# A delta-rule kernel: products of the solved group's last two channel blocks dealt out between value projections instead of a block behind them

## The chip, the cores and the metric

The kernel runs on one core of one Trainium2 chip. The metric is the device time of one execution in microseconds (us); lower is better. The core has five engines with queues of their own: TensorE (PE, with its weight loads shown as PEld), VectorE (DVE), ScalarE (ACT), GpSimd (POOL) and SyncE (SP), which issues the transfers.

## The reference, cut to what matters

A residual block over x of 128 sequences x 32 tokens x 512 channels: a cross attention, then a delta-rule attention with its MLP, then a quantised gated MLP. The change lies in the delta-rule attention:

```python
q = silu(silu(_causal_dwconv(h @ Wq.T, conv_q)))
k = silu(silu(_causal_dwconv(h @ Wk.T, conv_k)))
v = silu(silu(_causal_dwconv(h @ Wv.T, conv_v)))
q, k = _l2norm(q), _l2norm(k)          # per head: 32 heads of 16 channels
beta = jax.nn.sigmoid(h @ Wbeta.T)
# per head, over the 32 tokens of a sequence, S starting at 0:
err = S @ kt - vt
S = S - bt * err * kt^T
o = S @ qt
x = x + _rms(o, out_norm_w) @ Wout.T
```

## The kernel before

The program has four phases, one after the other: attention, delta, MLP and the last gated MLP. The delta phase treats the 4096 tokens in eight groups of 512 (16 sequences). The recurrence of a group is written as a triangular system: products of keys give the matrix L, products of queries and keys the matrix A, and U solves L U = V step by step over the 32 tokens. The outputs are then products of A and U.

The phase is a pipeline over `k` from -1 to 8, written out by hand as one order for each engine. In step `k`, group `g = k + 1` is projected, convolved and normalised (`nxt`), group `k` is turned and solved (`cur`), and the outputs of group `k - 1` are made (`prev`). All three flags hold in the six steps k = 1 to 6. Groups have four channel blocks `c` of 128 channels.

On PE a step with all three goes: transposes of V and L of group k, transposes of the rows of group g, `project` for q and k of block 0, transposes of U, `betas`, q and k of block 1, q and k of blocks 2 and 3, the four value projections with `powers` (sums of squares of q and k) between them, and then `spreads(g, 0)`, `power`, `spreads(g, 1)`, `total`, `out(k, 0)` and the four `gram(g, c)` with the rest of `out` and `spreads` among them. A `project` is four matmuls of 128x128 by 512 columns into one bank. `outer(k, c)` is the product of A and U for one channel block, 128 matmuls of 32x32 by 32 columns into one bank; its argument `parts` picks eighths of it. The float32 matmuls show as two records each in the trace, so a `project` is 8 records, an `outer` 256 and an eighth of it 32.

A project with `beside=(k, c)` issues one eighth of `outer(k, c)` behind each of its four matmuls. Before, q and k of block 2 carry `outer(k, 0)` in this way and q and k of block 3 carry `outer(k, 1)`. `outer(k, 2)` and `outer(k, 3)` are a block behind `powers(k, 3)`.

`spreads(g, 0)` waits for `stat_ready`, the norms. They come about as follows: `powers` sums squares into the bank `ss`; ACT takes the square root in `roots(k)` (line 1095), which in its queue stands behind the first taps of the last value projections and the two SiLUs of the first pair of value blocks (`silus_v(g, 0)`); DVE then takes the reciprocal and two small operations in `norms(k)` (lines 1236, 1238, 1241), behind the convolution of the last value block. After `norms`, DVE does one step of the solve (s = 8, lines 1271 and 1273) and then `scale(g, 0)`, which reads what `spreads(g, 0)` wrote.

DVE's solve has 31 steps for each group; steps 0 to 11 stand among the convolutions and scales of group g, and steps 12 to 30 follow `scale(g, 3)` in one run. The solve of the next group can begin only when the last one is done, since both use the one L buffer.

The copies of the `outer` banks on ACT (`outer(k, 2)`, `outer(k, 3)`, lines 1080 and 1081) stand behind `roots(k)`. `power(k)` on PE waits for all four.

Of the kernel before, what the change touches and what calls it, by code (L numbers as in the profile page):

```python
# [9 lines left out]
DC = D // P  # L10
# [649 lines left out]
def delta_phase(nc, x1, hrow, wq, wk, wv, wbeta, wout, conv, vecs, consts, om, spent):  # L660
# [5 lines left out]
    for g in range(NG):  # L666
        early += [f"{g}.h{c}" for c in range(DC)] + [f"{g}.{i}{c}" for c in range(DC) for i in "qk"]
        early += [f"{g}.v{c}" for c in range(DC)]
        for what in ("S0", "S1", "G0", "S2", "G1", "S3", "G2", "G3"):
            c = what[1]  # L670
            early += ([f"{g}.r{i}{c}" for i in "kqb"] if what[0] == "S" else
                      [f"{g}.gram{c}.{j}" for j in range(BG)])
    for k in range(-1, NG + 1):
        prev, cur, nxt = k >= 1, 0 <= k < NG, k + 1 < NG
# [7 lines left out]
    with ExitStack() as stack:  # L682
# [130 lines left out]
        def _(pe):  # L813
# [4 lines left out]
            def turned(k, name, src):  # L818

                p, full = R.open(pe, 0, f"{k}.{name}")  # L820
                for j in range(SB):
                    mm = pe.transpose(p[:, j * P:(j + 1) * P], src(int(name[1:]) * SB + j), ident[:])
                mm.then_inc(full, 1)

            def rows(g):
                for c in range(DC):
                    p, full = E.open(pe, 0, f"{g}.h{c}")
                    for t in range(TG):
                        if c == 0:
                            pe.wait_ge(hn_ready, g * TG + t + 1)  # L830
                        mm = pe.transpose(p[:, t * P:(t + 1) * P], xg[:, t, c * P:(c + 1) * P], ident[:])
                    mm.then_inc(full, 1)

            def betas(k):
                p, full = R.open(pe, 0, f"{k}.beta")
                for c in range(DC):
                    mm = pe.matmul(p[2 * NH:3 * NH, :], w_b[:, c, :], hT[:, c, :], start=(c == 0), stop=(c == DC - 1))
                mm.then_inc(full, 1)

            def project(g, name, c, beside=None):  # L840

                p, full = E.open(pe, 0, f"{g}.{name}{c}")
                i = "qkv".index(name)
                for n in range(DC):
                    mm = pe.matmul(p[:], w_qkv[:, i, n, c * P:(c + 1) * P], hT[:, n, :],  # L845
                                   start=(n == 0), stop=(n == DC - 1))
                    if n == DC - 1:
                        mm.then_inc(full, 1)
                    if beside is not None:
                        outer(beside[0], beside[1], (DC * i + n,))  # L850

            def powers(k, c):

                g = k + 1
                if c == 0:
                    R.open(pe, 0, f"{k}.ss")
                p, full = R.banks[R.at[f"{k}.ss"][0]], R.full[R.at[f"{k}.ss"][0]]
                pe.wait_ge(sq_ready, g * DC + c + 1)
                for i in range(2):
                    mm = pe.matmul(p[i * NH:(i + 1) * NH, :], heads[:, c, :], sq[:, c % 2, i, :],  # L860
                                   start=(c == 0), stop=(c == DC - 1), skip_group_check=True)
                mm.then_inc(sq_used if c < DC - 1 else full, 1)

            def spreads(g, c):
                if c == 0:
                    pe.wait_ge(stat_ready, 2 * (g + 1))
                for name in "kqb":
                    i = "qkb".index(name)
                    p, full = E.open(pe, 0, f"{g}.r{name}{c}")
                    pe.matmul(p[:], spread[i * NH:(i + 1) * NH, c, :], stat[i * NH:(i + 1) * NH, :],  # L870
                              start=True, stop=True).then_inc(full, 1)
# [17 lines left out]
            def outer(k, c, parts=range(2 * DC)):  # L889

                if parts[0] == 0:
                    R.open(pe, 0, f"{k}.O{c}")
                p, full = R.banks[R.at[f"{k}.O{c}"][0]], R.full[R.at[f"{k}.O{c}"][0]]
                A = Am[(k - 1) % 2]
                for b in range(2 * parts[0], 2 * parts[-1] + 2):
                    for e in range(2):
                        u = c * UC + 2 * b + e
                        for q in range(4):
                            rows_ = slice(q * S, (q + 1) * S)
                            mm = pe.matmul(p[rows_, b * S:(b + 1) * S], Us[rows_, u, :], A[rows_, u, :],  # L900
                                           start=(e == 0), stop=(e == 1), skip_group_check=True)
                if b == GB - 1:
                    mm.then_inc(full, 1)

            def power(k):

                pe.wait_ge(osq_ready, DC * k)
                p, full = R.open(pe, 0, f"{k}.power")
                for c in range(DC):
                    mm = pe.matmul(p[c * S:(c + 1) * S, :], ones[:], osq[:, c, :], start=True, stop=True,  # L910
                                   skip_group_check=True)
                mm.then_inc(full, 1)

            def total(k):
                R.used(pe, 0, f"{k}.power")
                p, full = R.open(pe, 0, f"{k}.total")
                for t in range(TG):
                    mm = pe.matmul(p[:, t:t + 1], osq[:, 0, t * P:(t + 1) * P], fourth[:], start=True, stop=True)
                mm.then_inc(full, 1)
# [13 lines left out]
            for k in range(-1, NG + 1):  # L933
                prev, cur, nxt = k >= 1, 0 <= k < NG, k + 1 < NG
                g = k + 1
                if cur:
                    pe.wait_ge(vt_ready, DC * (k + 1))
                    for i in range(NV):
                        turned(k, f"V{i}", lambda d: vt[:, :, d])
                    E.used(pe, 0, f"{k}.gram{DC - 1}.{BG - 1}")  # L940
                    for i in range(LE):
                        turned(k, f"L{i}", lambda t: Gs[:, t, :])
                if nxt:
                    rows(g)
                if cur:
                    for i in range(LE, NL):
                        turned(k, f"L{i}", lambda t: Gs[:, t, :])
                if nxt:
                    E.used(pe, 0, f"{g}.h{DC - 1}")
                    for name in "qk":  # L950
                        project(g, name, 0)
                if prev:
                    pe.wait_ge(sub, (S - 1) * k)
                    pe.wait_ge(pool_sub, (S - 1) * k)
                    for i in range(NV):
                        turned(k, f"U{i}", lambda d: Uf[(k - 1) % 2][:, :, d])
                if nxt:
                    betas(k)
                    for name in "qk":
                        project(g, name, 1)  # L960
                if prev:
                    for i in range(NV):
                        R.used(pe, 0, f"{k}.U{i}")
                    pe.wait_ge(ah_ready, (S - 1) * k)
                if nxt:
                    for name in "qk":
                        project(g, name, 2, (k, 0) if prev else None)
                    powers(k, 0)
                    for name in "qk":
                        project(g, name, 3, (k, 1) if prev else None)  # L970
                    project(g, "v", 0)
                    powers(k, 1)
                    project(g, "v", 1)
                    powers(k, 2)
                    project(g, "v", 2)
                    project(g, "v", 3)
                    powers(k, 3)
                elif prev:
                    outer(k, 0)
                    outer(k, 1)  # L980
                if prev:
                    outer(k, 2)
                    outer(k, 3)
                if nxt:
                    spreads(g, 0)
                if prev:
                    power(k)
                if nxt:
                    spreads(g, 1)
                if prev:  # L990
                    total(k)
                    out(k, 0)
                if nxt:
                    gram(g, 0, (k, 1) if prev else None)
                    spreads(g, 2)
                    gram(g, 1, (k, 2) if prev else None)
                    spreads(g, 3)
                    gram(g, 2, (k, 3) if prev else None)
                    gram(g, 3)
                elif prev:  # L1000
                    for t in range(1, TG):
                        out(k, t)
# [1173 lines left out]
```

## Time and profile before

| | |
|---|---|
| median of 3 runs | 3256.35 us (3254.93 to 3263.09) |
| the profiled execution's own time | 3251.3 us |
| its span in the trace | 3249.3 us |
| mean granted TensorE clock | 0.934 |
| PE busy in the span | 2897.0 us, 89% |
| DVE busy | 1944.5 us, 60% |
| ACT busy | 1462.6 us, 45% |
| delta phase in the trace, about | 604 to 1760 us |

The span is counted from the first to the last instruction of the profiled execution. Busy PE means that matmuls are in flight, whether at the full or at the half clock; the granted clock of a stretch tells these apart (1.00 is 2.4 GHz, 0.50 is 1.2 GHz).

### The profile page before, as it was taken

The page shows a single profiled execution, that of the slowest core. Times are in us where ns is not written, and L with a number is a line of the kernel's source. Part 1 is how long each engine was busy: PE and PEld are TensorE (multiplying, and loading weights), DVE is VectorE, ACT ScalarE, POOL GpSimd, SP SyncE. Part 2 cuts the span into 40 slices and gives each one's busy share as a digit, 9 for nine tenths or more (in the row PEclk, how much of TensorE's full clock was granted, in tenths as well). Part 3 has the DMA queues.
Part 4 walks back from the last instruction along what each step waited for, and adds up shares of the span by engine and source line. Part 5 has one row for each costly group of instructions (what it writes and reads, how often), then busy time and mean ns, then how long its engine had stood idle before and what let it go on. Part 6 is the DMA issues. An engine that isn't in the chain of part 4 may idle for free. (4 is left out here: it accounts for less than half of the span.)

```text
span 3249.3 us, 65853 instructions
## 1 busy us (share of the span) xinstructions
PE 2897.0 (89%) x26552; PEld 1541.2 (47%) x26552; DVE 1944.5 (60%) x2956; ACT 1462.6 (45%) x2438; POOL 1007.6 (31%) x710
## 2 busy tenths in 40 slices
PE   6999999587899988999844999999999699999997
PEld 3444444244454444444423444444444366666665
DVE  3444444259977978779891444445442466666665
ACT  2222222376665766757612422222222366666665
POOL 0000000125725527255290000000000267777776
PEclk9999999788989989989866999999999899999999
DMA  6998898200000000000003132322200111111010
GB/s 241 334 336 309 301 332 271 87 14 1 2 27 8 22 28 2 27 9 21 15 15 119 56 117 78 104 91 91 98 33 27 63 36 39 39 39 39 33 42 30
DMA packets 126423, 290.19 MB, mean 89 GB/s; under 512 B 30496, under 2 KB 35360, under 8 KB 122112
## 3 DMA queue, kind: packets, MB, share of 16 engines
q1 hardware_dynamic: 122752, 261.91, 23.0%
q10 hardware_dynamic: 3456, 25.17, 2.3%
q8 instruction: 165, 2.70, 0.4%
q14 instruction: 50, 0.41, 0.0%
HBM read 245.02 MB, written 42.01 MB: 88 GB/s over the span
## 5 line engine op out<-in xcount | busy, mean ns | idle before, releaser
L803 POOL TENSOR_TENSOR b_tmp<-b_L,b_U 128x496 f32<-128x496 f32 (+30 forms) x248 | 252.1, 1017 | 558.6 <-ACT b_L L1040 539.8
L1984 POOL TENSOR_TENSOR d_zb<-d_za 128x1024 f32<-128x1024 f32 x32 | 75.3, 2353 | 1047.0 <-DVE d_za L2040 1047.0
L845 PE MATMUL b_e<-b_hT,b_wqkv 128*128 128x512 f32 x768 | 367.8, 615 | 3.9 <-DVE b_raw L1223 3.1
L1273 DVE TENSOR_TENSOR b_U<-b_U,b_tmp 128x1488 f32<-128x1488 f32 (+30 forms) x248 | 282.2, 1138 | 8.6
L1271 DVE TENSOR_TENSOR b_tmp<-b_L,b_U 128x1488 f32<-128x1488 f32 (+30 forms) x248 | 265.3, 1070 | 32.3 <-ACT b_L L1040 26.4
L805 POOL TENSOR_TENSOR b_U<-b_U,b_tmp 128x496 f32<-128x496 f32 (+30 forms) x248 | 271.7, 1096 | 19.4
L1493 PE MATMUL c_r<-c_hT,c_g_pair 128*128 128x512 f16 x1056 | 255.5, 394 | 13.1 <-DVE c_hT L1658 13.1
L1223 DVE SCALAR_TENSOR_TENSOR b_raw<-b_e,b_cw,b_raw 128x496 f32<-128x496 f32 (+2 forms) x288 | 204.3, 717 | 99.2 <-ACT b_raw L1057 90.9
L1667 DVE SCALAR_TENSOR_TENSOR c_av<-c_r,c_sg 128x512 f32<-128x512 f32 x88 | 60.8, 691 | 305.3 <-PE c_r L1493 248.1
L1493 PE MATMUL c_r<-c_hT,c_u_pair 128*128 128x512 f16 x1056 | 242.7, 379 | 0.0
L1493 PE MATMUL c_d<-c_d_pair,c_aT 128*128 128x512 f16 x1056 | 241.0, 379 | 0.0
L1849 PE MATMUL d_m<-s_region,d_xiT 128*128 128x512 bf16 x1024 | 228.3, 381 | 3.7 <-ACT d_xiT L1963 2.4
L845 PEld LDWEIGHTS b_e<-b_hT,b_wqkv 128*128 128x128 f32 x768 | 136.7, 191 | 159.4 <-issue 150.0
L1493 PEld LDWEIGHTS c_r<-c_hT,c_g_pair 128*128 128x128 f16 x1056 | 105.7, 101 | 146.6 <-issue 16.3
L1580 ACT ACTIVATE c_sg<-c_r 128x512 f32<-128x512 f32 x88 | 52.5, 597 | 263.7 <-PE c_r L1493 263.6
L900 PE MATMUL b_r<-b_A,b_Up 32*32 32x32 f32 x8192 | 110.5, 209 | 62.6 <-issue 59.0
L900 PEld LDWEIGHTS b_r<-b_A,b_Up 32*32 32x32 f32 x8192 | 94.9, 122 | 145.0 <-issue 145.0
L1493 PEld LDWEIGHTS c_r<-c_hT,c_u_pair 128*128 128x128 f16 x1056 | 103.6, 98 | 125.5 <-issue 1.6
L1493 PEld LDWEIGHTS c_d<-c_d_pair,c_aT 128*128 128x128 f16 x1056 | 103.3, 98 | 124.6 <-DVE c_aT L1672 0.5
L1849 PEld LDWEIGHTS d_m<-s_region,d_xiT 128*128 128x128 bf16 x1024 | 100.2, 98 | 126.5 <-ACT d_xiT L1963 3.3
L1584 ACT CAST c_aT<-c_av 128x512 f16<-128x512 f32 x88 | 54.3, 617 | 230.6 <-DVE c_av L1667 230.6
L1934 ACT ACTIVATE d_sg<-d_m,d_gsc 128x512 f32<-128x512 f32 x128 | 87.6, 684 | 151.8 <-DVE d_fac L2060 132.0
(229 smaller groups left out, 5486.1 us busy)
## 6 DMA issues: line engine op xcount, KB each, us to landing
a_cT<-in_ctxT SPq DMA_DIRECT2D x128, 512.0 KB, 9.6
a_cn<-in_ctx SPq DMA_DIRECT2D x128, 512.0 KB, 8.6
a_x_ln<-in_x SPq DMA_DIRECT2D x8, 1024.0 KB, 15.7
a_cw<-in_ctx SPq DMA_DIRECT2D x128, 64.0 KB, 9.2
a_x_res<-in_x SPq DMA_DIRECT2D x32, 256.0 KB, 11.1
x<-a_x_out SPq DMA_DIRECT2D x32, 256.0 KB, 10.9
b_xg<-x SPq DMA_DIRECT2D x8, 1024.0 KB, 5.4
om<-b_hT SPq DMA_DIRECT2D x32, 256.0 KB, 2.0
```

The lines of the kernel that those rows point to most:

```text
L803: nc.gpsimd.tensor_tensor(tmp[:, QV, s + 1:S, :], lo, us, ALU.mult).then_inc(pool_prod, 1)
L805: nc.gpsimd.tensor_tensor(U[:, QV, s + 1:S, :], U[:, QV, s + 1:S, :], tmp[:, QV, s + 1:S, :], ALU.subtract).then_inc(pool_sub, 1)
L845: mm = pe.matmul(p[:], w_qkv[:, i, n, c * P:(c + 1) * P], hT[:, n, :], start=(n == 0), stop=(n == DC - 1))
L900: mm = pe.matmul(p[rows_, b * S:(b + 1) * S], Us[rows_, u, :], A[rows_, u, :], start=(e == 0), stop=(e == 1), skip_group_check=True)
L1223: ins = V.scalar_tensor_tensor(acc[:, :, j:S], src[:, :, 0:S - j], cw[:, i, c, TAPS - 1 - j:TAPS - j], acc[:, :, j:S], ALU.mult, ALU.add)
L1271: V.tensor_tensor(tmp[:, 0:QV, s + 1:S, :], lo, us, ALU.mult).then_inc(prod, 1)
L1273: V.tensor_tensor(U[:, 0:QV, s + 1:S, :], U[:, 0:QV, s + 1:S, :], tmp[:, 0:QV, s + 1:S, :], ALU.subtract).then_inc(sub, 1)
L1493: mm = pe.matmul(out, x, y, start=start and i == 0, stop=stop and i == 2)
L1667: V.scalar_tensor_tensor(av[:], p[:], AS / (WS * HS), sg[:, f % 2, :], ALU.mult, ALU.mult)\
L1849: mm = pe.matmul(p[:], xiT[:, c, :], w[:, c, j * 512:(j + 1) * 512], start=(c == 0), stop=(c == DC - 1))
L1934: A.activation(sg[:, j % 2, :], p[:], ACT.Silu, scale=gsc[:, 0:1]).then_inc(free, 1)
L1984: nc.gpsimd.tensor_tensor(o[:, :, 0, :], a[:, :, 0, :], a[:, :, 1, :], ALU.add).then_inc(bf, 1)
```

## The change

`project` maps its argument to an eighth of `outer` in another way, so that the value projections can carry one too, and the four value projections are given `beside`: blocks 0 and 1 carry `outer(k, 2)`, blocks 2 and 3 carry `outer(k, 3)`. The block of both behind `powers(k, 3)` stays only in steps without a next group (k = 7 and 8). Nothing else changes on any engine.

```diff
@@ project @@
                     if beside is not None:
-                        outer(beside[0], beside[1], (DC * i + n,))
+                        outer(beside[0], beside[1], (DC * (i if i < 2 else c % 2) + n,))
@@ PE's order @@
                     powers(k, 0)
                     for name in "qk":
                         project(g, name, 3, (k, 1) if prev else None)
-                    project(g, "v", 0)
+                    project(g, "v", 0, (k, 2) if prev else None)
                     powers(k, 1)
-                    project(g, "v", 1)
+                    project(g, "v", 1, (k, 2) if prev else None)
                     powers(k, 2)
-                    project(g, "v", 2)
-                    project(g, "v", 3)
+                    project(g, "v", 2, (k, 3) if prev else None)
+                    project(g, "v", 3, (k, 3) if prev else None)
                     powers(k, 3)
                 elif prev:
                     outer(k, 0)
                     outer(k, 1)
-                if prev:
                     outer(k, 2)
                     outer(k, 3)
                 if nxt:
```

## Rows read from the trace of the kernel before

**Rows 1.** The page's first line.
```profile
span 3249.3 us, 65853 instructions
```

**Rows 2.** Windows of step k = 3: length, busy time (records) by engine, clock, DMA.
```profile
1134.83:1152.10 17.27, 17.27 (x53) 6.26 (x44) 13.17 (x16) 10.44 (x14) 15.70 (x21) 1.00 0.00 1
1152.10:1164.66 12.56, 6.62 (x514) 6.17 (x512) 10.38 (x10) 8.17 (x9) 9.66 (x18) 0.67 0.02 4
1164.66:1178.66 14.00, 14.00 (x40) 5.54 (x37) 11.14 (x15) 7.49 (x9) 0.00 (x0) 0.56 0.01 2
1178.66:1205.53 26.87, 26.87 (x422) 13.87 (x421) 13.20 (x17) 15.73 (x31) 0.00 (x0) 1.00 0.09 32
```

**Rows 3.** Timeline of DVE in step k = 3 and PE later: start, length, idle before.
```profile
1188.24 0.69 DVE L1250 TENSOR_TENSOR b_raw<-b_raw,b_e 128x512 f32<-128x512 f32 x1 [9.99 <-PE b_e L870]
...
1227.47 1.71 DVE L1271 TENSOR_TENSOR b_tmp<-b_L,b_U 128x1488 f32<-128x1488 f32 x1 [0.55 <-ACT b_L L1040]
...
1620.49 3.66 PE L822 MATMUL b_r<-b_ident,b_U 128*128 128x128 f32 x16 [10.69 <-DVE b_U L1273]
```

**Rows 4.** Timeline of PE: value projections, powers and the block.
```profile
1134.83 3.70 PE L845 MATMUL b_e<-b_hT,b_wqkv 128*128 128x512 f32 x8
1138.46 1.05 PE L860 MATMUL b_r<-b_vt,b_heads 128*32 128x512 f32 x4
1139.44 3.70 PE L845 MATMUL b_e<-b_hT,b_wqkv 128*128 128x512 f32 x8
...
1152.10 1.99 PE L900 MATMUL b_r<-b_A,b_Up 32*32 32x32 f32 x213
```

**Rows 5.** Timeline of PE: eighths of an outer beside q and k of block 2.
```profile
1111.88 0.45 PE L900 MATMUL b_r<-b_A,b_Up 32*32 32x32 f32 x32
1112.26 1.12 PE L845 MATMUL b_e<-b_hT,b_wqkv 128*128 128x512 f32 x2
...
1121.95 0.45 PE L900 MATMUL b_r<-b_A,b_Up 32*32 32x32 f32 x32
```

**Rows 6.** Windows of the six blocks: their sum, nothing but the block in each.
```profile
sum 68.90, PE 37.38 PEld 35.07 DVE 61.18 ACT 48.79 POOL 47.14; mean PE 6.23 PEld 5.84 DVE 10.20 ACT 8.13 POOL 7.86
```

**Rows 7.** Timeline of ACT and DVE in step k = 3: from the last projection to the norms.
```profile
1151.23 0.69 ACT L1057 ACTIVATE b_raw<-b_e,b_cw 128x512 f32<-128x512 f32 x1 [2.75 <-PE b_e L845]
...
1155.26 0.59 ACT L1095 ACTIVATE b_stat<-b_r 64x512 f32<-64x512 f32 x1
...
1155.92 3.33 DVE L1236 RECIPROCAL b_stat<-b_stat 64x512 f32<-64x512 f32 x1
...
1159.74 0.42 DVE L1241 TENSOR_SCALAR b_stat<-b_stat 64x512 f32<-64x512 f32 x1
1160.08 1.29 DVE L1271 TENSOR_TENSOR b_tmp<-b_L,b_U 128x1104 f32<-128x1104 f32 x1
```

**Rows 8.** Timeline of PE in steps k = -1 and 0, which have no outer.
```profile
659.78 1.05 PE L860 MATMUL b_r<-b_vt,b_heads 128*32 128x512 f32 x4
668.84 6.85 PE L870 MATMUL b_e<-b_stat,b_spread 32*128 32x512 f32 x12 [8.01 <-DVE b_stat L1241]
...
776.72 7.28 PE L870 MATMUL b_e<-b_stat,b_spread 32*128 32x512 f32 x12 [12.21 <-DVE b_stat L1241]
```

**Rows 9.** Windows from `spreads(g, 0)` to `gram(g, 0)`, steps k = 1, 6, sum of six.
```profile
895.82:911.11 15.29, 15.29 (x39) 5.47 (x37) 11.77 (x16) 7.49 (x9) 0.92 (x2) 0.52 0.00 1
...
1561.69:1572.15 10.46, 10.46 (x41) 3.82 (x37) 8.44 (x12) 5.87 (x8) 0.67 (x2) 0.79 0.01 2
sum 78.32, PE 78.32 PEld 28.91 DVE 61.91 ACT 43.31 POOL 1.59; mean PE 13.05 PEld 4.82 DVE 10.32 ACT 7.22 POOL 0.26
```

**Rows 10.** Windows around the waits of steps k = -1 and 0.
```profile
664.00:668.84 4.84, 0.00 (x1) 0.00 (x1) 4.18 (x3) 3.90 (x4) 0.00 (x0) 0.59 0.00 0
668.84:678.40 9.56, 9.56 (x66) 4.67 (x70) 6.47 (x10) 4.00 (x4) 0.00 (x0) 0.50 0.01 2
...
776.72:787.30 10.58, 10.57 (x72) 4.81 (x76) 10.41 (x13) 2.48 (x3) 5.14 (x11) 0.50 0.00 0
```

## The prediction, made before the changed kernel had run

> **What bounds the kernel now.** The page gives the whole: 3249.3 us of span [rows 1]. The change touches six steps of the delta phase (k = 1 to 6), so I read one of them, k = 3, first in windows cut where PE's work changes, then in the timelines of PE, ACT and DVE.
>
> The windows show PE without a gap in the value projections (17.27 us, clock 1.00), then a block of 12.56 us in which PE is busy for only 6.62 us, then 14.00 us at a clock of 0.56, then 26.87 us at full clock [rows 2]. The block is `outer(k, 2)` and `outer(k, 3)`: 512 records, in bursts, the first 213 of them in 1.99 us [rows 4]; the timeline puts the gaps between bursts down to "issue", so PE waits there for nothing that the trace names. The clock falls to its lower level of 1.2 GHz in the block and comes back late in the 14 us behind it.
>
> Who sets the length of a step? Two loops lock. DVE waits for PE in the middle of the step, for instance 9.99 us for `spreads(g, 2)`; then it runs solve steps 12 to 30 with no wait, and the next solve starts 0.55 us after that end [rows 3]. PE in its turn needs the end of the solve for the transposes of U: where it has no projections to fill the time (k = 7), it waits 10.69 us for it [rows 3]. In k = 1 to 6 the path is therefore: end of solve, PE's projections, block, spreads, grams, `spreads(g, 3)`, `scale(g, 3)`, run of DVE, end of solve. What delays `gram(g, 0)` delays PE's solid 26.87 us behind it, then DVE's run, and so the step. ACT and POOL have room. I count from the start of the value projections to `gram(g, 0)` and take a shift there in full, six times.
>
> **The change, part by part.**
>
> *Removed: the block behind `powers(k, 3)`.* Six blocks sum to 68.90 us [rows 6], 11.48 each. From the start of the value projections to `spreads(g, 0)` it is 17.27 + 11.48 = 28.75 us on average before.
>
> *Added: an eighth of an outer behind each of 16 value matmuls.* The same pattern stands beside q and k. There the eighths start 10.07 us apart over seven rounds, 1.44 us a round, 0.38 us of it until the next projection starts [rows 5]. Without them a value block takes 3.63 us up to the `powers` and the `powers` 0.98 us [rows 4]. Taking three such `powers`, 2.95 us, from 17.27 [rows 2] leaves 14.32 us, 0.895 a matmul. With the eighths: 16 x 1.44 + 2.95 = 25.99 us, so 8.72 us more than before. By PE's own work alone the change would gain 11.48 - 8.72 = 2.76 us a step.
>
> That price is one of q and k projections; it could be otherwise beside v. From below: 32 records at the rate of the first burst (1.99 us for 213) are 0.30 us, so 1.19 us a round; from above: at the block's mean (12.56 us for 512) 0.79 us, so 1.68 a round. I take 1.44, the row of the same shapes, same operands and same weights' layout.
> The Trainium skill (TensorEngine Tiling, Key Properties) says that a change of tiling mode, unlike a change of tile, drains TensorE; that speaks against dealing out and against the lower price. The trace agrees in direction: 1.44 - 0.895 = 0.55 us for 32 records that need 0.30 in a burst. The page prices no drain, so the sum goes by the rows.
>
> *The wait that appears.* In k = 3 `spreads(g, 0)` starts the moment the block ends, but its input was not much earlier. The last value projection ends at 1151.12; ACT's tap starts at 1151.23, then come two SiLUs, a table load and the root at 1155.26; DVE's reciprocal (3.33 us) starts at 1155.92, and the last small operation ends at 1159.74 + 0.42 = 1160.16 [rows 7]. That chain is 9.04 us, all behind the last projection, and the block covered it. In step k = -1, with no outer, the same chain is bare: projection ends at 659.78, `spreads` starts at 668.84, 9.06 us, with PE idle for 8.01 [rows 8]. The change keeps this chain and starts it later. The last value bank is full at 25.99 - 0.98 (`powers`) - 0.38 (last eighth) = 24.63 us; `spreads(g, 0)` can start at 24.63 + 9.06 = 33.69. PE will be idle for 33.69 - 25.99 = 7.7 us. Could DVE be later than this? In k = 0 the wait is 12.21 us, since its convolutions lag; in k = 3 it lags less, it waits for ACT's taps of v0 and v3 by then, and slower projections give it more room. I add nothing.
>
> The shift of `spreads(g, 0)` is 33.69 - 28.75 = +4.94 us a step.
>
> *The ACT copies.* `outer(k, 3)` on ACT still stands behind `roots` and the second pair of SiLUs. It will end some 5.5 us behind the root, about 1 us after `spreads(g, 0)` starts, and those last about 2 us; `power` needs it only then. Nothing. On DVE, solve step 8 (from 1160.08 in k = 3, [rows 7]) ran in PE's block; now it runs after the norms and before `scale(g, 0)`. In k = 0 it stands just so, and both spreads take 7.28 us there against 6.85 in k = -1, where there is no solve [rows 8]: at most 0.4 us. SP, POOL and their queues are not touched; the banks of O2 and O3 were freed by earlier copies.
>
> *The clock.* From `spreads(g, 0)` to `gram(g, 0)` took 78.32 us in six steps, 13.05 each, between 10.46 at a clock of 0.79 and 15.29 at 0.52 [rows 9]. It would be tempting to count the low clock as gained with the block. But an idle PE loses it as well: in k = -1 the clock is at 0.50 soon after 664, and stays there for 9.56 us after work begins again; in k = 0 for 10.58 us [rows 10]. After a wait of 7.7 us most of these 13 us will run at 1.2 GHz as before. I keep 13.05: shift nothing, bounds -2.6 and +2.2.
> The Trainium skill (TensorE: Matmul & The Clock Gate, HAM oscillation) warns of idle gaps between bursts for this reason. A clock kept up would make the stretch nearer to 10.46, which is the second rival below.
>
> **Sum.** +4.94 us x 6 = +29.6 us. On the profiled execution: 3249.3 + 29.6 = 3278.9 us of span, or 3280.9 for its own time of 3251.3. That execution is 5 us under the median of the runs shown; on the median, 3256.35 + 29.6 = 3286.0 us.
>
> **The rivals.**
>
> *A, the forecast, 0.72.* The norms' chain is bare, the clock is low behind it. +29.6; with the post-wait stretch between its bounds, 6 x (4.94 - 2.6) = +14 to 6 x (4.94 + 2.2) = +43. Own range 3270 to 3299.
>
> *B, the clock comes back early or stays, 0.10.* For it: the block of small matmuls is gone, and PE works solidly up to the wait. Against it: [rows 10], twice. Each step gains about 2.6 us of the 4.94: +14 us, 3270. Still slower.
>
> *C, the dealt eighths cost less beside v, 0.09; not slower.* Its place is the 16 rounds; its price 1.19 us a round. Then v is full at 16 x 1.19 + 2.95 - 0.98 - 0.3 = 20.7 us, spreads start at 29.8, +1.0 a step: +6 us, within what a measurement of this kernel can tell from no change, 0.3% or 10 us. It decides below about 1.24 us a round; below 1.13 the change would win. Against it: 1.44 held over all rounds beside q and k.
>
> *D, a gain, 0.05.* PE needs only its own order: `spreads` would follow `powers` at 25.99, -2.76 a step, and with the clock kept -5.4: -17 to -32 us. It would need norms that do not wait for the last projection. Against it: even with the root taken at once at the end of `powers`, root, reciprocal and two small operations take 0.59 + 3.33 + 0.42 + 0.42 = 4.8 us.
>
> *E, the shift is absorbed elsewhere, 0.04.* The solve's end might be fixed by DVE alone. DVE waits 9.99 us for PE at one place, which speaks against it. 0, no change.
>
> **How the numbers follow.** Slower: A and B, 0.82. Within 0.3%: C and E, 0.13. Faster: D, 0.05. The predicted time is A's. From below, the range takes in B and the near edge of C, 3267 (+11); from above, the worst clock, 3299. That leaves out D, E and most of C.
>
> **What would show it.** Value projections of 26 us with eighths at 1.44 us; a wait of PE before `spreads(g, 0)` of 7 to 8 us, released by DVE's line 1241, in six steps; no issue gaps there in k = 1 to 6; a clock of about 0.5 in the 9 us after it; steps 5 us longer between `gram(g, 0)` of successive groups. Wrong if that wait is under 3 us, if the round is nearer 1.2 us, or if the clock stays at 1.00 across the wait.

## The result: slower by about 1%

The changed kernel takes 3288.11 us, median of 4 runs (3286.82 to 3291.06). In the same set of runs the kernel before takes 3257.93 us (4 runs). The ratio is 1.0092, 95% interval 1.0075 to 1.011: 30 us slower. Run again later, beside 17 runs of the kernel before (median 3251.76), the changed kernel gave 3288.28 and a ratio of 1.0115 (1.0097 to 1.0133): 36.5 us. The changed kernel repeats within a few microseconds; the kernel before spreads from 3241 to 3263 over all sets of runs. The prediction was 3286, +29.6.

The profiled execution of the changed kernel took 3287.66 us, with a span of 3285.6 us, 36.3 us over that of before [rows 1]:

```profile
span 3285.6 us, 65853 instructions
```

The windows of step k = 3, cut where PE's work changes as in [rows 2]: the value stage with its eighths, PE's wait, the stretch from `spreads(g, 0)` to `gram(g, 0)`, and the grams. The numbers are length, busy time (records) of PE, PEld, DVE, ACT and POOL, granted clock, DMA.

```profile
1143.29:1169.25 25.96, 25.96 (x564) 10.65 (x556) 14.63 (x17) 10.81 (x14) 19.09 (x36) 1.00 0.01 3
1169.25:1176.94 7.69, 0.07 (x2) 0.00 (x0) 5.95 (x7) 7.43 (x9) 0.00 (x0) 0.76 0.00 0
1176.94:1191.65 14.71, 14.71 (x37) 5.69 (x37) 13.62 (x17) 7.61 (x10) 0.00 (x0) 0.55 0.00 1
1191.65:1218.52 26.87, 26.87 (x422) 13.87 (x421) 13.20 (x17) 15.73 (x31) 0.00 (x0) 1.00 0.09 32
```

The block of 12.56 us has gone, the value stage has grown from 17.27 to 25.96 us, and in the block's place PE does nothing for 7.7 us. The grams are the same to the hundredth. The timeline of ACT, DVE and PE at that wait (start, length, idle time before) shows what it is for:

```profile
1167.99 0.69 ACT L1056 ACTIVATE b_raw<-b_e,b_cw 128x512 f32<-128x512 f32 x1 [5.07 <-PE b_e L845]
...
1170.73 1.28 ACT L1094 ACT_TABLE_LOAD   x1
1172.02 0.59 ACT L1094 ACTIVATE b_stat<-b_r 64x512 f32<-64x512 f32 x1
...
1172.64 3.34 DVE L1235 RECIPROCAL b_stat<-b_stat 64x512 f32<-64x512 f32 x1 [1.61 <-ACT b_stat L1094]
...
1176.94 2.08 PE L870 MATMUL b_e<-b_stat,b_spread 32*128 32x512 f32 x6 [7.62 <-DVE b_stat L1240]
```

It is the chain of [rows 7], with the same durations, 8.3 us later in the step: the root starts 28.7 us after the start of the value stage, where it was 20.4. DVE, which in [rows 7] went from one piece of work to the next, now itself waits 1.61 us for the root. The waits of PE over k = 1 to 6 (us in total, times, longest) say that all six steps have it, 7.63 us each:

```profile
PE b_e L870 <- DVE b_stat L1240: 45.8, 6, 7.6
```

Last, the stretch behind it, the six windows as in [rows 9] (first, and the sum of six):

```profile
898.24:912.36 14.12, 14.12 (x37) 5.51 (x37) 13.62 (x17) 7.60 (x10) 0.00 (x0) 0.57 0.00 1
...
sum 86.44, PE 86.43 PEld 33.70 DVE 81.69 ACT 45.61 POOL 0.00; mean PE 14.41 PEld 5.62 DVE 13.62 ACT 7.60 POOL 0.00
```

It is 14.41 us a step where it was 13.05. Of the kernel before, two of six steps came out at 12.15 us and one at 10.46; of the changed one none is under 13.99.

### The profile page after: what moved, and what is told of

Read it like the earlier page. It is cut to its first block and busy times, and to the rows that moved or that the text cites. A ratio compares the mean times of both kernels' runs of the same rounds, so it can differ in the third digit from the quotient of the medians.

```text
span 3285.6 us, 65853 instructions
## 1 busy us (share of the span) xinstructions
PE 2922.6 (89%) x26552; PEld 1538.3 (47%) x26552; DVE 1944.9 (59%) x2956; ACT 1461.7 (44%) x2438; POOL 988.5 (30%) x710
## 5 line engine op out<-in xcount | busy, mean ns | idle before, releaser
L803 POOL TENSOR_TENSOR b_tmp<-b_L,b_U 128x496 f32<-128x496 f32 (+30 forms) x248 | 243.0, 980 | 615.0 <-ACT b_L L1039 596.1
L845 PE MATMUL b_e<-b_hT,b_wqkv 128*128 128x512 f32 x768 | 386.1, 622 | 4.3 <-DVE b_raw L1222 3.6
L805 POOL TENSOR_TENSOR b_U<-b_U,b_tmp 128x496 f32<-128x496 f32 (+30 forms) x248 | 262.0, 1057 | 19.4
L845 PEld LDWEIGHTS b_e<-b_hT,b_wqkv 128*128 128x128 f32 x768 | 129.3, 189 | 124.6 <-issue 111.4
L1056 ACT ACTIVATE b_raw<-b_e,b_cw 128x512 f32<-128x512 f32 x96 | 65.6, 685 | 216.9 <-PE b_e L845 216.8
```

The source lines that it names most:

```text
L803: nc.gpsimd.tensor_tensor(tmp[:, QV, s + 1:S, :], lo, us, ALU.mult).then_inc(pool_prod, 1)
L805: nc.gpsimd.tensor_tensor(U[:, QV, s + 1:S, :], U[:, QV, s + 1:S, :], tmp[:, QV, s + 1:S, :], ALU.subtract).then_inc(pool_sub, 1)
```

## The experiments

All were run beside the kernel before. The two positions given are counted from the start of the value stage in a step of the profiled execution (k = 3): the kernel before has `spreads(g, 0)` at 29.8 there (28.75 on average) and `gram(g, 0)` at 43.8 (41.8), the changed kernel has 33.65 and 48.4. One step can mislead, since the stretch before `gram(g, 0)` varies with the clock, so the last column has the mean of `gram(g, 0)` over k = 1 to 6.

| kernel | median us | before, same set | ratio (95%) | spreads | gram | gram, mean |
|---|---|---|---|---|---|---|
| e1, half dealt out | 3258.44 | 3252.21 | 1.0020 (1.0010 to 1.0029) | 29.6 | 42.0 | 43.0 |
| e2, a quarter dealt out | 3248.17 | 3252.21 | 0.9991 (0.9980 to 1.0002) | 28.3 | 42.0 | 41.1 |
| e3, filler in the wait | 3287.39 | 3252.21 | 1.0104 (1.0089 to 1.0119) | 33.7 | 47.7 | 47.7 |
| e4, norms early | 3267.85 | 3252.21 | 1.0050 (1.0036 to 1.0064) | 26.2 | 45.2 | 45.4 |
| e5, norms and scales early | 3225.65 | 3251.76 | 0.9920 (0.9905 to 0.9934) | 26.2 | 38.5 | 39.0 |
| e6, as e5, with the block | 3245.66 | 3251.76 | 0.9984 (0.9972 to 0.9996) | 29.3 | 39.7 | 42.7 |
| e7, as e5, out first | 3234.09 | 3251.76 | 0.9948 (0.9935 to 0.9962) | 26.2 | 39.3 | 39.5 |
| e8, changed kernel again | 3288.28 | 3251.76 | 1.0115 (1.0097 to 1.0133) | 33.6 | 48.4 | 48.1 |
| e9, filler in both places | 3270.59 | 3253.48 | 1.0059 (1.0042 to 1.0076) | 33.7 | 45.1 | 45.1 |
| e10, as e5, with a filler | 3214.63 | 3253.48 | 0.9884 (0.9866 to 0.9902) | 26.2 | 37.1 | 37.1 |

### How much is dealt out: e1 and e2

```diff
-                    project(g, "v", 2, (k, 3) if prev else None)
-                    project(g, "v", 3, (k, 3) if prev else None)
+                    project(g, "v", 2)
+                    project(g, "v", 3)
                     powers(k, 3)
+                    if prev:
+                        outer(k, 3)
```

> The changed kernel with outer(k, 3) put back as a block behind powers(k, 3); outer(k, 2) stays dealt out beside v0 and v1. Bare-chain theory: value stage 8 x 1.44 + 8 x 0.895 + 2.95 = 21.6 us, last value bank full at 20.65, so spreads(g, 0) at 20.65 + 9.06 = 29.7 us from the stage's start, 4 us earlier than in the changed kernel (33.7) and 1 us later than before (28.75). The block of 256 records takes about 5 us, so PE still waits some 3 us. Time: 24 to 30 us under the changed kernel, 0 to +10 us against before. If it were the dealt pattern itself that costs (no wait): half of the change's +30 us, +15 us against before.

The second kernel deals out less still:

```diff
                     project(g, "v", 0, (k, 2) if prev else None)
-                    project(g, "v", 1, (k, 2) if prev else None)
+                    project(g, "v", 1)
...
                     powers(k, 3)
+                    if prev:
+                        outer(k, 2, range(DC, 2 * DC))
+                        outer(k, 3)
```

> The changed kernel with only four eighths dealt out (first half of outer(k, 2) beside v0); the other twelve are a block behind powers(k, 3). Bare-chain theory: chain ready at 16.29 + 4 x 0.545 + 9.06 = 27.5 us, block ends at 17.27 + 2.18 + about 8.6 = 28.05 us: the two meet, no wait of PE on the norms longer than 0.5 us, spreads(g, 0) 0.7 us earlier than before in each of six steps. Time: -4 us against before, -10 to +3. If dealing out costs by itself, in proportion: +7 us.

PE's timeline of e1 in step k = 3:

```profile
1156.94 1.05 PE L860 MATMUL b_r<-b_vt,b_heads 128*32 128x512 f32 x4
...
1166.01 2.08 PE L870 MATMUL b_e<-b_stat,b_spread 32*128 32x512 f32 x6 [3.60 <-DVE b_stat L1242]
```

9.07 us lie between the end of the last projection (where `powers` starts) and `spreads`, whatever PE does in between: the chain. The wait is 3.6 us here and 2.9 to 5.7 over the six steps, 7.6 with all dealt out. In e2 four of the six steps have no such wait; the other two wait 2.5 and 1.8 us, where I had expected none over 0.5, because the block takes a different time from step to step. e1 came out 6.2 us slower than before, inside the bound of the bare-chain theory and below the 15 us of its rival; it is 30 us under the changed kernel, so the second half of the eighths cost nearly all of the loss: `spreads(g, 0)` is 4.06 us earlier in every step, and the stretch behind it is 13.44 us on average where the changed kernel has 14.41, because the clock came back early in three of the six. A price for each eighth could not give that: the loss is a chain that runs out of cover. e2's -4 us is what was expected, but its interval just includes no change.

### The wait or the clock: e3 and e9

```diff
                     powers(k, 3)
+                    if prev:
+                        p, _ = R.open(pe, 0, f"{k}.total")
+                        for i in range(8):
+                            pe.matmul(p[:], w_qkv[:, 2, i % DC, 0:P], hT[:, i % DC, :], start=True, stop=True)
```

> The changed kernel plus eight 128x128x512 matmuls a step behind powers(k, 3), written to a bank that total(k) overwrites later, so nothing of the result depends on them; they take 7.2 us and fill the wait for the norms. It tells the wait from the clock. Theory: spreads(g, 0) does not move (33.7 us, the chain sets it), but the clock stays at 1.00, and the stretch up to gram(g, 0) shrinks from 14.4 us (changed kernel) to about 11.5: -17 us against the changed kernel, +13 against before. If the stretch were set by DVE and ACT and not by the clock: no change from the changed kernel. If the wait were not the chain's: +7 us a step more.

The median did not change (3287.39; the five runs spread from 3280.20 to 3290.99, and the profiled one is the slowest). The windows of e3 in step k = 3: the filler, the first 5.1 us of the stretch behind, and its rest.

```profile
1171.09:1178.79 7.70, 7.14 (x19) 2.96 (x17) 5.96 (x7) 7.44 (x9) 0.00 (x0) 1.00 0.00 0
1178.79:1183.90 5.11, 4.32 (x18) 1.04 (x18) 5.01 (x7) 2.44 (x5) 0.00 (x0) 1.00 0.01 2
1183.90:1192.78 8.88, 8.85 (x19) 4.29 (x19) 8.60 (x11) 5.26 (x6) 0.00 (x0) 0.62 0.01 3
```

The filler did keep the clock at 2.4 GHz through the wait, and `spreads(g, 0)` did not move. But then the clock fell to its lower level anyhow, 5.1 us after `spreads(g, 0)` began (6.1 to 6.6 in the other five steps), in a stretch where PE has a few matmuls of 32 rows and waits for `scale(g, 0)`. So the stretch took 14.1 us all the same, and my expectation, which took the idle wait for the only cause, missed: it said 17 us under the changed kernel, and it was under 1. e9 fills that place too:

```diff
                 if prev:
                     power(k)
+                    if nxt:
+                        p, _ = R.open(pe, 0, f"{k}.total")
+                        for i in range(4):
+                            pe.matmul(p[:], w_qkv[:, 2, i % DC, 0:P], hT[:, i % DC, :], start=True, stop=True)
```

> The kernel of e3 (changed kernel with eight filler matmuls behind powers(k, 3)) plus four more of them between power(k) and spreads(g, 1), where PE waits for scale(g, 0). In e3 the clock stayed at 1.00 through the wait for the norms but fell some 5 us after spreads(g, 0) began, in the sparse stretch. Theory (that sparse stretch loses the clock by itself): filled too, the clock stays at 1.00 up to gram(g, 0), and the stretch shrinks from 14.1 us to 11.5 to 12: 12 to 16 us under the changed kernel's 3288, that is +20 to +24 against before. Rival (the stretch is DVE's and ACT's, not the clock's): no change from the changed kernel, or slower by the filler.

```profile
1161.44:1169.12 7.68, 7.12 (x18) 2.94 (x16) 5.93 (x7) 7.42 (x9) 0.00 (x0) 1.00 0.00 0
1169.12:1180.59 11.47, 11.35 (x44) 4.54 (x44) 11.26 (x16) 6.84 (x10) 0.00 (x0) 1.00 0.01 3
```

Now the clock is at 1.00 in the stretch too, and it takes 11.47 us in every one of the six steps. The time is 17 us under e3's and 18 under the changed kernel's. The lower clock is thus worth 14.41 - 11.47 = 2.9 us a step in the changed kernel, 17.6 us in six steps. It costs mostly in the second half of the stretch: in k = 3 `out(k, 0)` takes 5.19 us in e3 and 3.68 in e9, while `scale(g, 0)`, for which PE waits in the first half, ends 5.8 us after the start of `spreads(g, 0)` in the changed kernel, in e3 and in e9 alike. So the full clock in the first half alone gained e3 only 0.35 us a step. The wait for the norms is still there in e9, and it keeps the kernel 17 us slower than before.

### The chain moved: e4, e5, e7

e4 leaves all eighths where the change put them and takes the norms off the last projection (the diffs are cut to the lines that move, engine by engine):

```diff
 PE
                     project(g, "v", 2, (k, 3) if prev else None)
+                    powers(k, 3)
                     project(g, "v", 3, (k, 3) if prev else None)
-                    powers(k, 3)
 ACT
                     tap_first(g, "v", 2)
-                    tap_first(g, "v", 3)
-                    silus_v(g, 0)
                     roots(k)
+                    silus_v(g, 0)
+                    tap_first(g, "v", 3)
 DVE
                         convolve(g, "v", 2)
+                        norms(k)
                     if nxt and s == 7:
                         convolve(g, "v", 3)
-                        norms(k)
```

> The changed kernel with the norms' chain moved ahead of the last value projection on all engines: powers(k, 3) before v3 on PE, roots before the SiLUs of v and the tap of v3 on ACT, norms right behind the convolution of v2 on DVE. All sixteen eighths stay dealt out. Bare-chain theory: the wait of 7.6 us before spreads(g, 0) goes nearly away (start at about 26.1 us instead of 33.7). What is late next: DVE, which now has solve 7, the convolution of v3 and solve 8 between the norms and scale(g, 0), so spreads(g, 1) ends at about 38.3 us and gram(g, 0) starts at 43 to 45.6 us, against 48.1 in the changed kernel and 41.8 before. Time: 15 to 31 us under the changed kernel, 0 to +14 us against before. If the dealt pattern itself cost the time: no change from the changed kernel.

PE's timeline of e4:

```profile
1158.41 1.14 PE L870 MATMUL b_e<-b_stat,b_spread 32*128 32x512 f32 x6
1166.54 1.94 PE L910 MATMUL b_r<-b_M,b_ones 128*32 128x512 f32 x8 [6.99 <-ACT b_M L1080]
```

`spreads(g, 0)` follows the last eighth without a wait, 7.5 us earlier than in the changed kernel, and the kernel is 20 us faster than the changed one. It is still 15.6 us slower than before, just beyond the +14 expected. The positions were as expected, but another engine than the one I named was also late: `power(k)` waits 6.99 us for ACT's copies of `outer(k, 3)`, which stand behind SiLUs that wait for DVE's convolution of v3. e5 moves both:

```diff
 DVE
                         norms(k)
-                    if nxt and s == 7:
                         convolve(g, "v", 3)
-                    if nxt and s in (8, 9, 10, 11):
-                        scale(g, s - 8)
+                    if nxt and s in (6, 7, 10, 12):
+                        scale(g, (6, 7, 10, 12).index(s))
 ACT
                 if prev:
                     outer(k, 2)
+                    outer(k, 3)
                 if nxt:
                     silus_v(g, 1)
                 if prev:
-                    outer(k, 3)
                     power(k)
```

> The kernel of e4 with what stood in its way moved: on DVE the norms, the convolution of v3 and scale(g, 0) all come in slot s = 6, scale(g, 1) in slot 7, scale(g, 2) in slot 10 and scale(g, 3) in slot 12, so the solve steps fall into DVE's waits for PE; on ACT the copies of outer(k, 2) and (k, 3) stand before the second pair of SiLUs of v. Theory (the dealt pattern is a gain of 2.8 us a step on PE, the bare chain and DVE's order took it): spreads(g, 0) at 26 us, scale(g, 0) done at 31.5, gram(g, 0) at 37.4 to 40 us, against 41.8 before: -11 to -26 us against before. Rival (dealing out costs in itself): not faster than before.

26 us faster than before, 63 us faster than the changed kernel, with all sixteen eighths dealt out. Not all of this comes from the six steps. From the value stage of k = -1 to that of k = 1, where no eighth is dealt out, the kernels with early norms (e4 to e7, e10) take 220.5 to 220.8 us and the others 224.9 to 227.4: early norms shorten the bare waits of [rows 8] too, by some 4 us. So e5 against the kernel before mixes the deal-out with the move of the norms; only e6 takes them apart.

e7 then tried to fill the rest of PE's wait with work that is there anyway:

```diff
+                if prev:
+                    total(k)
+                    out(k, 0)
                 if nxt:
                     spreads(g, 1)
-                if prev:
-                    total(k)
-                    out(k, 0)
-                if nxt:
                     gram(g, 0, (k, 1) if prev else None)
```

> The kernel of e5 with total(k) and out(k, 0) ahead of spreads(g, 1) on PE, so that 4 us of matmuls that need nothing of DVE fill PE's wait for scale(g, 0). Expected gram(g, 0) at 34 to 37 us from the start of the value stage: 6 to 18 us under e5. If the clock or DVE holds that stretch: same as e5.

```profile
1150.23 1.43 PE L910 MATMUL b_r<-b_M,b_ones 128*32 128x512 f32 x8 [1.30 <-ACT b_M L1079]
1153.11 1.86 PE L918 MATMUL b_r<-b_fourth,b_M 128*128 128x1 f32 x8 [1.45 <-ACT b_M L1085]
1154.83 5.06 PE L928 MATMUL b_r<-b_wo,b_xg 128*128 128x512 f32 x8
1159.82 1.13 PE L870 MATMUL b_e<-b_stat,b_spread 32*128 32x512 f32 x6
```

A miss: 8 us slower than e5. `total` needs ACT's copy of `power`, so one wait was traded for another, the lower clock came in there, and `spreads(g, 1)` now comes so late that DVE waits 5.07 us for it before `scale(g, 1)`. `gram(g, 0)` came at 39.3 us, where 34 to 37 had been expected.

### The price of the block against the eighths: e6

e5's kernel with this in PE's order:

```diff
-                    project(g, "v", 3, (k, 3) if prev else None)
+                    project(g, "v", 3)
+                    if prev:
+                        outer(k, 2)
+                        outer(k, 3)
```

and v0 to v2 without `beside`.

> The kernel of e5 with outer(k, 2) and outer(k, 3) as a block behind the last value projection, as before the change. With the norms early nothing is hidden behind the block, so its price against the dealt eighths stands alone: theory 11.5 - 8.7 = 2.8 us a step, 17 us slower than e5, part of which DVE may hide (spreads start at 28.75, but DVE is done with the convolution of v3 earlier): 6 to 17 us slower than e5. Rival: dealing out costs in itself, then this one is the faster of the two.

e6 is 20.0 us slower than e5, 3.3 us a step (k = 3 alone shows less, since in e6 the clock came back early there). Expected were 6 to 17, so this is a miss in size. The six traced steps say where it lies: `spreads(g, 0)` comes at 28.98 us on average against 26.18 in e5, which is PE's own 2.8 us a step, 16.8 in all; the stretch behind it takes 13.69 us against 12.87, at a mean clock of 0.59 against 0.83, another 4.9 us, which the expectation left out. With the norms out of the way, dealing out is the faster of the two orders.

### The changed kernel again, and the fastest version: e8, e10

> The changed kernel once more, on the chip of e5 to e7, to have its ratio with more runs: +25 to +36 us against before, ratio 1.008 to 1.011.

+36.5 us and a ratio of 1.0115, just above what was expected (+25 to +36).

e10 is e5 with the second filler of e9, of two matmuls:

> The kernel of e5 (norms and scales early, all eighths dealt out) plus two filler matmuls between power(k) and spreads(g, 1). In e5 the clock falls in that stretch and out(k, 0) takes 5.4 us where it takes 3.6 at full clock. If the filler keeps the clock up: stretch from 12.3 to about 10.7 us, 6 to 10 us under e5 (3216 to 3220). If the clock falls all the same: the filler costs 0 to 1 us a step, e5's time or up to 6 us more.

```profile
1142.58:1153.51 10.93, 9.63 (x40) 3.78 (x40) 10.41 (x15) 9.16 (x13) 0.00 (x0) 1.00 0.00 1
```

The same stretch of e5 took this:

```profile
1145.05:1157.37 12.32, 10.53 (x37) 4.03 (x37) 11.79 (x16) 10.56 (x14) 0.00 (x0) 0.86 0.01 1
```

3214.63 us, ratio 0.9884: 39 us faster than before and 11 us faster than e5, a little more than expected, by matmuls that compute nothing that is used. The clock stays at 1.00, and `gram(g, 0)` comes at 37.1 us.

## Why the prediction was right, point by point

*PE sets the length of the step.* Right. The grams after `gram(g, 0)` took 26.87 us before and after, and shifts of `gram(g, 0)` came out in the time: in the changed kernel six spreads at 33.65 and 86.44 us behind them, less six times 28.75 and 78.32, are 37.5 us, against 36.3 in the spans. That puts rival E, a shift absorbed elsewhere, out. The two numbers agree more closely than they should, though: from the value stage of k = 1 to `gram(g, 0)` of k = 6 the changed kernel's trace is 39.9 us longer (6.9 us longer between successive grams, predicted 5), and the part ahead of the first value stage, which the change does not touch, happened to be 4.2 us shorter in that execution (639.4 us against 643.6).

*The eighths at 1.44 us a round.* Right. The value stage is 25.96 us, predicted 25.99. Rival C, a lower price beside v, is out: PE's timeline shows the rounds 1.44 us apart.

```profile
1163.57 0.45 PE L900 MATMUL b_r<-b_A,b_Up 32*32 32x32 f32 x32
1163.95 1.13 PE L845 MATMUL b_e<-b_hT,b_wqkv 128*128 128x512 f32 x2
1165.01 0.45 PE L900 MATMUL b_r<-b_A,b_Up 32*32 32x32 f32 x32
```

*The chain of the norms, laid bare.* Right, and the heart of it: `spreads(g, 0)` at 33.65 us against 33.69, a wait of 7.63 against 7.7, released by the operation named (line 1241 before, 1240 in the changed file), in all six steps. e1 and e2 move the cover and the wait follows; e4 and e5 move the chain and the wait goes. That also turns rival D from argument into measurement: with norms that do not wait for the last projection, the dealt pattern is a gain (e5 against e6).

*The ACT copies and solve step 8, put at nothing.* Right for ACT: its last copy ends 1.2 us after `spreads(g, 0)` starts, and `power` follows the spreads without a wait. On DVE, solve step 8 delays `scale(g, 0)` by 0.26 us a step (it starts 2.54 us after `spreads(g, 0)` where it was 2.28), within the 0.4 allowed.

*The stretch up to `gram(g, 0)`, "I keep 13.05".* The mechanism was right, the size off: 14.41 us, so 1.36 us a step or 8.2 us in all were missing from the sum, inside the bound of +2.2 given. About 0.26 us of it can be solve step 8; the rest goes with the clock. The kernel before had steps in which the clock was back early ([rows 9], 10.46 us at 0.79); behind a wait of the same length each time, the changed kernel had none: in all six the clock fell 3.7 to 5.1 us before `spreads(g, 0)` and came back 11.9 to 13.4 us after it. I had taken the mean of lucky and unlucky steps for what a step costs that always begins at the lower clock.

*The clock's cause.* I put the low clock down to the block before and to the wait after. e3 shows that neither is needed: the sparse stretch loses it by itself, and of the kernels with late norms only e9, with both places filled, keeps it. Rival B's premise, a clock that stays or comes back early, never occurred in the changed kernel's trace. It can happen behind such a wait, though: in e1, behind waits of 3.4, 3.6 and 5.7 us, it came back within 3.7 us of `spreads(g, 0)` in three of six steps. What decides this from step to step is not shown.

*The forecast in the whole.* 3286.0 against a measured 3288.11. Part of this nearness is chance. The sum of steps was 8 us short of the traced 37.5, and between the two traces the forecast span, 3278.9, is 6.7 us under the measured 3285.6. But 3286.0 was counted from 3256.35, the median of three runs of the kernel before, and 17 later runs of it have a median of 3251.76, 4.6 us lower; the two errors nearly cancel. With more runs of before, the loss is 36.5 us, not 30.

What stays open is why the kernel before spreads over 20 us from run to run while the changed one and e10 hold within a few. The clock in the sparse stretch varies from step to step in one trace of the kernel before, and the mean clock of whole runs goes with their time: of the 23 runs beside e1 to e4 the fastest (3242.41 us) has 0.936 and the slowest (3261.04 us) 0.928. That ties the spread to the clock; it does not say what moves the clock.

## What to carry to other kernels

A block of "inefficient" work may be the cover of a latency chain on other engines. Before it is dealt out, measure the chain from its last input to its consumer (here 9.06 us, bare in the steps of the pipeline's start) and see what is left on top of it. If the gain is real, move the chain's start first, then the work: the same deal-out cost 30 to 36 us with the norms late, and was worth 20 us with them early (e5 against e6). And look at what stands in the queues behind the new free place: each removed wait showed the next one, on ACT in e4, on DVE behind it.

## What the runs showed of the hardware that was not expected

- The lower clock came in a stretch that follows 7 us of solid matmuls at full clock, with PE shown busy for 4.32 of the 5.11 us before it fell (e3, k = 3). Busy time in the trace was no sign here that the clock would stay.
- Two matmuls of no use, 1.9 us of PE time a step in a place where it waited anyway, went with a clock of 1.00 in the stretch of all six steps, where e5 has 0.76 to 0.86, and took 11 us off the kernel (e10 against e5).
- A table load on ACT was followed by its function 1.29 us after its start (1170.73 to 1172.02), with no further pause between.
